# A DLRM tower on one core: in the first block all 26 tables are gathered, and lookups begin with the second block

## The chip, the cores and the metric

One core of one Trainium2 chip. The metric is the device time of one execution in microseconds, the median over timed runs. The core's engines are TensorE (PE in the profile), VectorE (DVE), ScalarE (ACT), GpSimd (POOL) and SyncE (SP), which run their own instruction streams and meet at semaphores.

## The reference, cut to what matters

```python
# ids: [2048, 26]; tables f: [V_f, 128], V_f = 1000 (seven of them), 1250, 12500 or 125000
e = stack([tbl_f[ids[:, f]] for f in range(26)], axis=1)          # [2048, 26, 128]
combined = concatenate((dense[:, None, :], e), axis=1)            # [2048, 27, 128]
inter = einsum('bfd,bgd->bfg', combined, combined)
pairs = inter[:, iu, ju]                                          # 351 pairs f < g
h = concatenate([dense, pairs, dense], axis=1)                    # [2048, 607]
h = maximum(h @ W_top1 + b_top1, 0.0)                             # 512
h = maximum(h @ W_top2 + b_top2, 0.0)                             # 256
y = h @ W_top3                                                    # [2048, 1]
```

Everything is float32.

## The kernel before, in words

The batch of 2048 is cut into 16 tiles of 128 samples; two tiles are a block (JT = 2, eight blocks). For each tile the kernel needs 27 slots in the tile `feats`: column 0 is the dense features, then seven small tables (1000 rows each), then nineteen large ones. Each slot holds, transposed, 128 dimensions by 128 samples.

The two kinds of table reach `feats` on different ways.

- Small tables, by lookup. The whole table is loaded once to SBUF (`load_table`, L181) in 125 partitions of eight rows, and split by ScalarE (`round_table`, L254) and VectorE (L391) into a rounded part `table_hi` and a remainder `table_lo`. For each block and small table, VectorE makes a one-hot tile of 1000 rows by 256 samples (`one_hot`, L338 to L345) from ids that SP has broadcast to all partitions (`load_wanted`, L174). TensorE multiplies the table with it in 16 matmuls (`look_up`, L419 to L432: eight chunks, two parts), and ScalarE copies the result from the PSUM bank `look` to `feats` (`empty_lookup`, L258). That makes 56 lookups (8 blocks x 7). There is one `look` bank, so lookup v waits until lookup v - 1 has been read; there are two one-hot tiles.
- Large tables, by gather. POOL issues one indirect DMA per tile and table (L248), 304 in all. It lands 128 rows, one per sample, in a slot of `rows`. Four gathers (at the end of a tile three) make a chunk, five chunks a tile, and chunk q = 5t + k uses slot q % 12. From the twelfth chunk on POOL waits until the chunk that held the slot has been turned (L246). TensorE turns a chunk with one transpose per table into a `turn` bank (`turn_rows`, L434 to L442; two banks), and ScalarE copies the bank to `feats` (`empty_turn`, L265).

The order of the work is written out by hand on each engine; there is no planner. Ahead of the tiles stands a start (PE at L497 to L502, ScalarE at L302 to L309, VectorE at L388 to L395, SP at L199 to L217): for k = 0 to 6 a table is rounded and looked up for block 0, and from k = 1 to 5 chunk k - 1 of tile 0 is turned between two lookups. So the start holds seven lookups and five chunks. SP issues the loads of the first four tables with their wanted ids, then the dense features of tile 0, part of W_top1, the other three tables, more wanted ids, and last the remaining weights. A load of wanted ids from the fifth on waits until an earlier one-hot has been made (L176), and everything behind it in SP's queue waits too. The raw tables land in the space of feature tiles 2 and 3.

Then follow 16 tiles of four segments each. In segment s of tile t TensorE does `products` (L444; 16 matmuls of 128 by 108, eight groups per bank), then one chunk of tile t + 1 (in the fourth segment two, L50), then in seven of the eight segments of a pair of tiles one lookup for the next block (`lookup_at`, L66), and one part of the MLP of tile t - 1: in segment 1 the pairs are turned (L461), in segment 2 and 3 the first and second layer (L469, L481), in segment 0 of the tile after that the third (L490). ScalarE reads products, chunks and lookups in the same order (`read_products`, L278). Products of a tile wait in segment 0 for all chunks and lookups of the tile and its dense column (L446 to L449). In the last two tiles there are no lookups; the last gather is issued during tile 12.

Of the kernel before, what the change touches and what calls it, by code (L numbers as in the profile page):

```python
# [7 lines left out]
I32 = mybir.dt.int32  # L8
# [19 lines left out]
ORDER = (0,) + tuple(1 + f for f in SMALL) + tuple(1 + f for f in LARGE)  # L28
LOOKUPS = BLOCKS * NS

# [35 lines left out]
def lookup_at(t, s):  # L66

    u = SEGS * (t % 2) + s
    return (t // 2 + 1) * NS + u if u < NS and t // 2 + 1 < BLOCKS else None


def arrivals(q):

    return sum(16 * CHUNK[i % NC][1] for i in range(q % SLOTS_OF_ROWS, q + 1, SLOTS_OF_ROWS))


def tower_program(nc, gather_ids, small_ids, dense_cols, dense_rows, small_tables, large_tables,
                  w_pairs, w_dense, w_dense2, w2, w3, b1, b2, y):
    ctx = ExitStack()
    with ctx:  # L80
# [3 lines left out]
        def sem(name):  # L84
            return ctx.enter_context(nc.semaphore(name))
# [9 lines left out]
        one = sb("one", [CP, 1])  # L95
        ids = sb("ids", [P, TILES, NG], I32)
        ident = sb("ident", [P, P])
        diag = [sb(f"diag{i}", [P, GROUPS * SLOTS]) for i in range(2)]
# [19 lines left out]
        ids_first_in = sem("ids_first_in")  # L118
        ids_rest_in = sem("ids_rest_in")
        gathered = [sem(f"gathered{i}") for i in range(SLOTS_OF_ROWS)]  # L120
        wanted_in = [sem(f"wanted_in{i}") for i in range(WANTED)]
# [41 lines left out]
        def raw_table(k):  # L163
            at = (2 + k % RAW // 2) * FT + k % 2 * CH * D
            return feats[0:CP, at:at + CH * D]

        def tail_bank(n):
            return prod[n // SEG_BANKS][:, (n % SEG_BANKS) * BANK:(n % SEG_BANKS) * BANK + P]
# [4 lines left out]
        def _(sp):  # L173
            def load_wanted(v):  # L174
                if v >= WANTED:
                    sp.wait_ge(onehot_ready, v - WANTED + 1)  # L176
                sp.dma_start(wanted[v % WANTED][:, :],
                             small_ids[v // NS:v // NS + 1, v % NS, :].broadcast_to([P, BS]))\
                    .then_inc(wanted_in[v % WANTED], 16)
# [53 lines left out]
        def _(gp):  # L233
# [5 lines left out]
            gp.wait_ge(ids_first_in, 16)  # L239
            for t in range(TILES):  # L240
                if t == 1:
                    gp.wait_ge(ids_rest_in, 16)
                for k, (g, m) in enumerate(CHUNK):
                    q = NC * t + k
                    if q >= SLOTS_OF_ROWS:
                        gp.wait_ge(turn_full, q - SLOTS_OF_ROWS + 1)  # L246
                    for f in range(m):
                        gp.indirect_dma_start(rows[:, q % SLOTS_OF_ROWS, f * D:(f + 1) * D], None, large_tables[g + f],  # L248
                                              bass.IndirectOffsetOnAxis(ap=ids[:, t, g + f:g + f + 1], axis=0))\
                            .then_inc(gathered[q % SLOTS_OF_ROWS], 16)  # L250

        @block.scalar
        def _(act):
# [4 lines left out]
            def empty_lookup(v):  # L258
                act.wait_ge(look_full, v + 1)
                at = v // NS % 2 * JT * FT  # L260
# [4 lines left out]
            def empty_turn(t, k):  # L265
                q, (g, m) = NC * t + k, CHUNK[k]
                act.wait_ge(turn_full, q + 1)
                nc.scalar.activation(slots_of(t)[:, 1 + NS + g:1 + NS + g + m, :],  # L268
                                     turn[q % 2][:, 0:m * P].rearrange("d (f b) -> d f b", f=m), ACT.Copy)\
                    .then_inc(turn_read, 1)  # L270
# [39 lines left out]

            for t in range(TILES):
                for s in range(SEGS):
# [3 lines left out]
                    if t + 1 < TILES:  # L316
                        for k in TURNS_AT[s]:
                            empty_turn(t + 1, k)
                        if s == 1:
                            place_dense(t + 1)  # L320
# [16 lines left out]
        def _(dve):  # L337
# [80 lines left out]
        def _(pe):  # L418
# [14 lines left out]

            def turn_rows(t, k):  # L434
                q, (g, m) = NC * t + k, CHUNK[k]
                pe.wait_ge(gathered[q % SLOTS_OF_ROWS], arrivals(q))
                if q >= 2:
                    pe.wait_ge(turn_read, q - 1)
                for f in range(m):
                    last = nc.tensor.transpose(turn[q % 2][:, f * P:(f + 1) * P],  # L440
                                               rows[:, q % SLOTS_OF_ROWS, f * D:(f + 1) * D], ident[:, :])
                last.then_inc(turn_full, 1)  # L442

            def products(t, s):  # L444
                m = SEGS * t + s
                if s == 0:  # L446
                    pe.wait_ge(turn_read, NC * (t + 1))
                    pe.wait_ge(look_read, NS * (t // 2 + 1))
                    pe.wait_ge(dense_placed, t + 1)  # L449
# [48 lines left out]
            pe.wait_ge(pads_ready, FEAT_TILES)  # L498
            for k in range(NS):
                look_up(k)  # L500
                if 1 <= k <= NC:
                    turn_rows(0, k - 1)  # L502

            for t in range(TILES):
                for s in range(SEGS):
# [3 lines left out]
                    if t + 1 < TILES:  # L509
                        for k in TURNS_AT[s]:  # L510
                            turn_rows(t + 1, k)
                    if (v := lookup_at(t, s)) is not None:
# [89 lines left out]
```

## Time and profile before

| | |
|---|---|
| median of three timed runs | 576.89 us (573.42 to 577.21) |
| profiled execution, its own time | 581.66 us |
| its span | 579.8 us |
| mean granted TensorE clock | 0.85 of full |
| busy PE, PEld, DVE, ACT, POOL | 407.9, 390.1, 212.6, 218.8, 297.6 us |
| matmuls | 3104 |
| DMA | 34.36 MB, mean 59 GB/s |

The profile shows one execution. PE is TensorE's matmul row, PEld its weight loads. A row of the timeline reads: start in us, duration in us, engine, line of the kernel, instruction, output<-input, count, and in brackets the idle time ahead of it and who ended it. Ends of matmuls are modelled. "remote" and "another core or an unknown queue" stand for a releaser that the profile could not name. A window over several instructions merges neighbours of one kind. Idle time of an engine off the critical path costs nothing.

### The profile page before, as it was taken

What the parts mean: (1) busy time and instruction counts of PE and PEld (TensorE: products, weight loads), DVE (VectorE), ACT (ScalarE), POOL (GpSimd) and SP (SyncE); (2) the same over time, 40 slices, a digit from 0 to 9 for tenths busy, and PEclk for the clock granted to TensorE, in tenths of its full rate; (3) what the DMA queues carried; (4) which work ended last, traced back from release to release, by engine and by line L of the source; (5) the groups of instructions that cost most, each with busy time, mean ns of one, the idle gap of its engine ahead of it and who ended that gap; (6) DMA issues with size and microseconds to landing.
All of it is one profiled execution on the core that took longest, in us unless ns stands there. A gap on an engine that the chain in (4) does not pass through costs nothing.

```text
span 579.8 us, 8030 instructions
## 1 busy us (share of the span) xinstructions
PE 407.9 (70%) x3104; PEld 390.1 (67%) x3104; DVE 212.6 (37%) x603; ACT 218.8 (38%) x452; POOL 297.6 (51%) x311
## 2 busy tenths in 40 slices
PE   1503027667859495987969595986949595899997
PEld 1502027667859495976859494976849494899995
DVE  5502027233434324453434323443433423371122
ACT  1201024444334342444335341444334352455641
POOL 5777746575555646474555636475554646400000
PEclk9766559897969788896979799896969898799998
DMA  8922215222112222222122212221121222100000
GB/s 190 245 63 59 54 35 167 64 68 55 53 48 55 52 53 56 55 69 52 45 63 54 57 49 59 51 69 51 46 60 50 50 57 63 41 6 1 2 1 1
DMA packets 24935, 34.36 MB, mean 59 GB/s; under 512 B 8808, under 2 KB 18552, under 8 KB 24898
## 3 DMA queue, kind: packets, MB, share of 16 engines
q0 software_dynamic: 9728, 19.94, 14.0%
q1 hardware_dynamic: 13090, 13.76, 9.1%
q8 instruction: 25, 0.41, 0.3%
q10 hardware_dynamic: 2080, 0.16, 0.3%
q14 instruction: 12, 0.10, 0.1%
HBM read 33.82 MB, written 0.01 MB: 58 GB/s over the span
## 4 chain that ended last, share of the span: by engine, by line
PE 58%; another core or an unknown queue 22%; ACT 9%; issue 8%; DMA 2%; DVE 1%; SPq 0%
PE prod L456 19%; PE look L429 19%; PE mlp L474 7%; PE mlp L485 4%; PE turn L440 4%; ACT feats L268 3%; ACT diag L283 3%; PE mlp L476 2%; DMA dense<-in_dense_rows 2%; ACT feats L261 1%; PE mlp L466 1%; PE prod L535 1%; ACT table_hi L256 1%; ACT y_sb L296 0%
## 5 line engine op out<-in xcount | busy, mean ns | idle before, releaser
L248 POOL DMA_INDIRECT rows<-in_tbl,ids x304 | 296.8, 976 | 206.9 <-PE turn L440 78.6
L429 PE MATMUL look<-onehot,table_hi 125*128 125x256 f32 x448 | 137.9, 334 | 138.6 <-ACT feats L261 105.6
L343 DVE TENSOR_SCALAR onehot<-wanted,row_no 125x256 fp32r<-125x256 int32 x448 | 132.9, 368 | 186.4 <-remote 150.4
L429 PEld LDWEIGHTS look<-onehot,table_hi 125*128 125x128 f32 x448 | 103.5, 231 | 144.0 <-issue 144.0
L456 PE MATMUL prod<-feats 128*128 128x108 f32 x1024 | 133.6, 283 | 16.5 <-issue 11.2
L283 ACT ACTIVATE diag<-prod 32x216 f32<-32x216 f32 x256 | 87.7, 343 | 148.4 <-PE prod L456 137.6
L456 PEld LDWEIGHTS prod<-feats 128*128 128x128 f32 x1024 | 127.2, 200 | 19.4 <-issue 11.7
L429 PE MATMUL look<-onehot,table_lo 125*128 125x256 f32 x448 | 131.9, 321 | 0.0
L429 PEld LDWEIGHTS look<-onehot,table_lo 125*128 125x128 f32 x448 | 104.1, 232 | 0.0
L268 ACT ACTIVATE feats<-turn 128x512 f32<-128x512 f32 (+1 forms) x80 | 79.5, 1032 | 41.7 <-remote 25.4
L261 ACT ACTIVATE feats<-look 128x256 f32<-128x256 f32 x56 | 34.9, 624 | 139.5 <-remote 116.1
L366 DVE TENSOR_SCALAR h<-mlp,b_sb 128x128 f32<-128x128 f32 x90 | 26.0, 345 | 147.9 <-PE mlp L476 101.8
L440 PE MATMUL turn<-ident,rows 128*128 128x128 f32 x304 | 48.7, 282 | 12.3 <-issue 12.3
L474 PE MATMUL mlp<-pairs_t,w_sb 117*128 117x128 f32 x360 | 50.2, 275 | 0.2 <-ACT pairs_t L290 0.2
L440 PEld LDWEIGHTS turn<-ident,rows 128*128 128x128 f32 x304 | 36.4, 147 | 17.8 <-issue 17.7
L474 PEld LDWEIGHTS mlp<-pairs_t,w_sb 117*128 117x128 f32 x360 | 45.0, 191 | 0.5 <-ACT pairs_t L290 0.4
L352 DVE STREAM_TRANSPOSE table<-diag 128x864 f32<-128x864 f32 x16 | 31.5, 1969 | 0.0
L485 PE MATMUL mlp<-h,w_sb 128*128 128x128 f32 x240 | 29.3, 275 | 0.0
L485 PEld LDWEIGHTS mlp<-h,w_sb 128*128 128x128 f32 x240 | 28.0, 192 | 0.0
L476 PE MATMUL mlp<-dense,w_sb 128*128 128x128 f32 x120 | 23.2, 274 | 0.0
L476 PEld LDWEIGHTS mlp<-dense,w_sb 128*128 128x128 f32 x120 | 18.2, 191 | 0.0
L391 DVE TENSOR_TENSOR table_lo<-feats,table_hi 125x1024 fp32r<-125x1024 f32 x7 | 8.6, 1227 | 19.7 <-issue 11.3
(39 smaller groups left out, 96.9 us busy)
## 6 DMA issues: line engine op xcount, KB each, us to landing
wanted<-in_small_ids SPq DMA_DIRECT2D x56, 128.0 KB
rows<-in_tbl,ids POOLq DMA_INDIRECT x304
feats<-in_tbl SPq DMA_DIRECT2D x7, 448.0 KB
dense<-in_dense_rows SPq DMA_DIRECT2D x16, 64.0 KB
w_sb<-in_w_pairs SPq DMA_DIRECT2D x1, 702.0 KB
w_sb<-in_w SPq DMA_DIRECT2D x1, 512.0 KB
feats<-in_tbl SPq DMA_DIRECT2D x7, 52.0 KB
w_sb<-in_w_dense SPq DMA_DIRECT2D x1, 256.0 KB
```

The costliest lines, as they stand in the source:

```text
L248: gp.indirect_dma_start(rows[:, q % SLOTS_OF_ROWS, f * D:(f + 1) * D], None, large_tables[g + f], bass.IndirectOffsetOnAxis(ap=ids[:, t, g ...
L261: nc.scalar.activation(feats[:, at:at + JT * FT].rearrange("d (b w) -> d w b", w=W)[:, 1 + v % NS, :], look[:, 0:BS], ACT.Copy)\
L268: nc.scalar.activation(slots_of(t)[:, 1 + NS + g:1 + NS + g + m, :], turn[q % 2][:, 0:m * P].rearrange("d (f b) -> d f b", f=m), ACT.Copy)\
L283: last = nc.scalar.activation(diag[t % 2][W * i:W * (i + 1), s * SEG_GROUPS * SLOTS:(s + 1) * SEG_GROUPS * SLOTS], prod_part(prod[s % 2], ...
L343: made = nc.vector.tensor_scalar(onehot[v % 2][:, c, :], wanted[v % WANTED][0:CP, :], row_no[:, c:c + 1], None, ALU.is_equal)
L352: nc.vector.transpose(by_row[:, :, 0:SLOTS].rearrange("p i j -> p j i"), diag[t % 2][:, :].rearrange("p (n j) -> p j n", j=SLOTS)).then_in ...
L429: last = nc.tensor.matmul(look[:, 0:BS], part[:, k, c * D:(c + 1) * D], onehot[v % 2][:, c, :], start=(c == 0 and part is table_hi), stop= ...
L440: last = nc.tensor.transpose(turn[q % 2][:, f * P:(f + 1) * P], rows[:, q % SLOTS_OF_ROWS, f * D:(f + 1) * D], ident[:, :])
L456: last = nc.tensor.matmul(prod[s % 2][:, to:to + GS * SLOTS], own, own.rearrange("d (s w) -> d s w", w=W)[:, :, 0:SLOTS], start=True, stop ...
L474: nc.tensor.matmul(mlp[:, n * P:(n + 1) * P], w1_sb[0:PR, c * H1 + n * P:c * H1 + (n + 1) * P], pairs_t[:, c * P:(c + 1) * P], start=(c == ...
L476: last = nc.tensor.matmul(mlp[:, n * P:(n + 1) * P], w1_sb[:, PC * H1 + n * P:PC * H1 + (n + 1) * P], dense[t % DENSE][:, :], start=False, ...
L485: last = nc.tensor.matmul(mlp[:, n * P:(n + 1) * P], w2_sb[:, c * H2 + n * P:c * H2 + (n + 1) * P], h1[:, c * P:(c + 1) * P], start=(c == ...
```

## The change

Lookups for block 0 are gone (`LOOKUPS` = 49, `lookup_at` numbers them from block 1). For tiles 0 and 1 POOL gathers the seven small tables as well, after the nineteen large ones: seven chunks a tile (4, 4, 4, 4, 3, 4, 3) in place of five. The list `CHUNKS` numbers all chunks in order; tiles 2 to 15 keep five. Two new loads on ScalarE's queue bring the ids of the small tables for tiles 0 and 1, one sample per partition. TensorE's start is seven chunks, each into a bank of its own: the two `turn` banks, the four halves of the `prod` banks, and `look`. ScalarE's start rounds all seven tables, places the dense column and empties the seven chunks. In tile 0 the chunks of tile 1 are spread over the segments as 1, 2, 2, 2; later tiles keep 1, 1, 1, 2. The loads of wanted ids in the start are three in place of ten. ScalarE waits before it empties the first lookup until all tables have been split, since the raw tables lie in the same space.

```diff
-LOOKUPS = BLOCKS * NS
+LOOKUPS = (BLOCKS - 1) * NS
...
-CHUNK = tuple((g, min(TB, NG - g)) for g in range(0, NG, TB))
-NC = len(CHUNK)
+FIRST_OF_LARGE = tuple((1 + NS + g, min(TB, NG - g)) for g in range(0, NG, TB))
+FIRST_OF_SMALL = tuple((1 + k, min(TB, NS - k)) for k in range(0, NS, TB))
+def chunks_of(t):
+    return FIRST_OF_LARGE + FIRST_OF_SMALL if t < JT else FIRST_OF_LARGE
+CHUNKS = tuple((t, *chunk) for t in range(TILES) for chunk in chunks_of(t))
...
-TURNS_AT = ((0,), (1,), (2,), tuple(range(3, NC)))
+def turns_at(t, s):
+    first, n = chunks_before(t), len(chunks_of(t))
+    ends = [n * (i + 1) // SEGS for i in range(SEGS)]
+    return range(first + (ends[s - 1] if s else 0), first + ends[s])
...
+        START_BANKS = [turn[0][:, :], turn[1][:, :], prod[0][:, 0:BANK], prod[0][:, BANK:], prod[1][:, 0:BANK],
+                       prod[1][:, BANK:], look[:, :]]
...
             for k in range(RAW):
-                load_wanted(k)
                 load_table(k)
+                if k < WANTED - 1:
+                    load_wanted(k)
...
             for k in range(RAW, NS):
-                load_wanted(k)
                 load_table(k)
-            for v in range(NS, NS + WANTED - 1):
-                load_wanted(v)
...
+            for q, (t, first, m) in enumerate(CHUNKS):
+                if q == chunks_before(1):
                     gp.wait_ge(ids_rest_in, 16)
+                if first < 1 + NS:
+                    gp.wait_ge(first_small_ids_in, 16 * JT)
+                if q >= SLOTS_OF_ROWS:
+                    gp.wait_ge(turn_full, q - SLOTS_OF_ROWS + 1)
+                for f in range(m):
+                    k = first - 1 + f
+                    rows_wanted = first_small_ids[:, t, k:k + 1] if k < NS else ids[:, t, k - NS:k - NS + 1]
+                    gp.indirect_dma_start(rows[:, q % SLOTS_OF_ROWS, f * D:(f + 1) * D], None,
+                                          (small_tables + large_tables)[k],
+                                          bass.IndirectOffsetOnAxis(ap=rows_wanted, axis=0))\
+                        .then_inc(gathered[q % SLOTS_OF_ROWS], 16)
...
+                if v == 0:
+                    act.wait_ge(lo_ready, NS)
...
+            for t in range(JT):
+                act.dma_start(first_small_ids[:, t, :], small_ids[0, :, t * P:(t + 1) * P].rearrange("k p -> p k"),
+                              allow_slow_non_contiguous=True).then_inc(first_small_ids_in, 16)
...
-            round_table(0)
+            for k in range(NS):
+                round_table(k)
             place_dense(0)
-            for k in range(NS):
-                if k + 1 < NS:
-                    round_table(k + 1)
-                empty_lookup(k)
-                if 1 <= k <= NC:
-                    empty_turn(0, k - 1)
+            for q in range(chunks_before(1)):
+                empty_turn(q)
...
             for k in range(NS):
-                one_hot(k)
+                if k == 1:
+                    one_hot(0)
                 dve.wait_ge(hi_ready, k + 1)
...
-            one_hot(NS)
...
                 pe.wait_ge(gathered[q % SLOTS_OF_ROWS], arrivals(q))
-                if q >= 2:
+                if q >= len(START_BANKS):
                     pe.wait_ge(turn_read, q - 1)
...
-            for k in range(NS):
-                look_up(k)
-                if 1 <= k <= NC:
-                    turn_rows(0, k - 1)
+            for q in range(chunks_before(1)):
+                turn_rows(q)
```

## Rows read from the trace of the kernel before

**Rows 1.** The page's slices: busy tenths in 40 slices of 14.5 us
```profile
PE   1503027667859495987969595986949595899997
...
POOL 5777746575555646474555636475554646400000
```

**Rows 2.** The costliest group of the page: busy, mean ns | idle before, releaser
```profile
L248 POOL DMA_INDIRECT rows<-in_tbl,ids x304 | 296.8, 976 | 206.9 <-PE turn L440 78.6
```

**Rows 3.** Stretches: length, busy (instructions) of PE, PEld, DVE, ACT, POOL, clock, DMA share, GB/s
```profile
5.30:30.00 24.70, 10.61 (x56) 10.02 (x56) 13.53 (x35) 5.92 (x8) 19.22 (x19) 0.86 0.99 242
30.00:75.30 45.30, 4.59 (x20) 4.24 (x20) 4.89 (x10) 2.84 (x4) 34.59 (x36) 0.56 0.22 57
...
185.40:218.00 32.60, 24.75 (x188) 23.79 (x187) 12.04 (x36) 12.84 (x27) 17.76 (x19) 0.84 0.21 54
...
513.20:535.30 22.10, 21.43 (x189) 20.86 (x187) 9.33 (x28) 12.75 (x27) 0.00 (x0) 1.00 0.00 1
```

**Rows 4.** Timeline of PE, 24 to 94 us
```profile
26.33 0.36 PE L429 MATMUL look<-onehot,table_hi 125*128 125x256 f32 x1 [0.71 <-issue]
...
28.32 0.60 PE L440 MATMUL turn<-ident,rows 128*128 128x128 f32 x4
44.78 0.55 PE L429 MATMUL look<-onehot,table_hi 125*128 125x256 f32 x1 [15.85 <-ACT feats L261]
...
82.65 0.55 PE L429 MATMUL look<-onehot,table_hi 125*128 125x256 f32 x1 [33.28 <-ACT feats L261]
...
93.36 2.01 PE L456 MATMUL prod<-feats 128*128 128x108 f32 x16 [0.75 <-issue]
```

**Rows 5.** Timeline of ACT, 29 to 82 us
```profile
29.30 1.05 ACT L256 ACTIVATE table_hi<-feats 125x1024 fp32r<-125x1024 f32 x1
44.02 0.61 ACT L261 ACTIVATE feats<-look 128x256 f32<-128x256 f32 x1 [13.67 <-remote]
53.84 1.02 ACT L268 ACTIVATE feats<-turn 128x512 f32<-128x512 f32 x1 [9.21 <-issue]
...
81.89 0.62 ACT L261 ACTIVATE feats<-look 128x256 f32<-128x256 f32 x1 [26.17 <-remote]
```

**Rows 6.** Timeline of POOL: gathers 1, 20, 26, 52 and 55
```profile
5.30 1.10 POOL L248 DMA_INDIRECT rows<-in_tbl,ids  x1 [3.72 <-DMA ids<-in_gather_ids]
...
30.94 1.49 POOL L248 DMA_INDIRECT rows<-in_tbl,ids  x1 [0.30 <-issue]
...
38.98 0.94 POOL L248 DMA_INDIRECT rows<-in_tbl,ids  x1 [0.30 <-issue]
...
71.82 0.94 POOL L248 DMA_INDIRECT rows<-in_tbl,ids  x1 [0.30 <-issue]
...
82.18 0.95 POOL L248 DMA_INDIRECT rows<-in_tbl,ids  x1 [6.92 <-remote]
```

**Rows 7.** Timeline of PE, ACT and POOL in tile 3, 181 to 200 us
```profile
181.84 1.60 POOL L248 DMA_INDIRECT rows<-in_tbl,ids  x1 [4.25 <-PE turn L440]
...
187.82 0.66 PE L440 MATMUL turn<-ident,rows 128*128 128x128 f32 x4
...
188.23 0.37 PE L429 MATMUL look<-onehot,table_hi 125*128 125x256 f32 x1
...
192.31 1.03 ACT L268 ACTIVATE feats<-turn 128x512 f32<-128x512 f32 x1 [2.57 <-remote]
...
199.43 0.61 ACT L261 ACTIVATE feats<-look 128x256 f32<-128x256 f32 x1 [6.09 <-remote]
...
199.89 1.05 POOL L248 DMA_INDIRECT rows<-in_tbl,ids  x1 [2.59 <-remote]
```

**Rows 8.** The chain that ended last: first and last of nine pieces alike
```profile
159.92 6.07 another core or an unknown queue
...
487.73 6.07 another core or an unknown queue
```

**Rows 9.** Gathers issued up to the first product of tile 2 (POOL alone)
```profile
0.00:151.30 151.30, 95.81 (x97) 0.77 0.39 97
```

**Rows 10.** DMA issues: queue, count, KB, median us to landing
```profile
ids<-in_gather_ids ACTq DMA_DIRECT2D x1, 142.5 KB, 6.0
```

More of the change, by code:

```diff
@@ L46, with chunks_before @@
 TB = 4
-CHUNK = tuple((g, min(TB, NG - g)) for g in range(0, NG, TB))
-NC = len(CHUNK)
-SLOTS_OF_ROWS = 12
-TURNS_AT = ((0,), (1,), (2,), tuple(range(3, NC)))
+FIRST_OF_LARGE = tuple((1 + NS + g, min(TB, NG - g)) for g in range(0, NG, TB))
[3 more added lines that the diff above has]
+CHUNKS = tuple((t, *chunk) for t in range(TILES) for chunk in chunks_of(t))
+SLOTS_OF_ROWS = 12
+def chunks_before(t):
+    return sum(len(chunks_of(i)) for i in range(t))
+def turns_at(t, s):
+    first, n = chunks_before(t), len(chunks_of(t))
+    ends = [n * (i + 1) // SEGS for i in range(SEGS)]
+    return range(first + (ends[s - 1] if s else 0), first + ends[s])
 PAIRS = SLOTS * (SLOTS - 1) // 2
@@ L68, in lookup_at @@
     u = SEGS * (t % 2) + s
-    return (t // 2 + 1) * NS + u if u < NS and t // 2 + 1 < BLOCKS else None
+    return t // 2 * NS + u if u < NS and t // 2 + 1 < BLOCKS else None
 def arrivals(q):
-    return sum(16 * CHUNK[i % NC][1] for i in range(q % SLOTS_OF_ROWS, q + 1, SLOTS_OF_ROWS))
+    return sum(16 * CHUNKS[i][2] for i in range(q % SLOTS_OF_ROWS, q + 1, SLOTS_OF_ROWS))
 def tower_program(nc, gather_ids, small_ids, dense_cols, dense_rows, small_tables, large_tables,
@@ L96, in tower_program @@
         ids = sb("ids", [P, TILES, NG], I32)
+        first_small_ids = sb("first_small_ids", [P, JT, NS], I32)
         ident = sb("ident", [P, P])
@@ L119, in tower_program @@
         ids_rest_in = sem("ids_rest_in")
+        first_small_ids_in = sem("first_small_ids_in")
         gathered = [sem(f"gathered{i}") for i in range(SLOTS_OF_ROWS)]
@@ L165, in raw_table, with turn_bank @@
             return feats[0:CP, at:at + CH * D]
+        START_BANKS = [turn[0][:, :], turn[1][:, :], prod[0][:, 0:BANK], prod[0][:, BANK:], prod[1][:, 0:BANK],
+                       prod[1][:, BANK:], look[:, :]]
+        def turn_bank(q):
+            return START_BANKS[q] if q < len(START_BANKS) else turn[q % 2]
         def tail_bank(n):
@@ L239, in _ @@
             gp.wait_ge(ids_first_in, 16)
-            for t in range(TILES):
-                if t == 1:
+            for q, (t, first, m) in enumerate(CHUNKS):
+                if q == chunks_before(1):
                     gp.wait_ge(ids_rest_in, 16)
[L243 to L250, printed above, removed]
+                if first < 1 + NS:
[9 more added lines that the diff above has]
+                        .then_inc(gathered[q % SLOTS_OF_ROWS], 16)
         @block.scalar
@@ L263, in empty_lookup, with empty_turn @@
                     .then_inc(look_read, 1)
-            def empty_turn(t, k):
-                q, (g, m) = NC * t + k, CHUNK[k]
+            def empty_turn(q):
+                t, first, m = CHUNKS[q]
                 act.wait_ge(turn_full, q + 1)
-                nc.scalar.activation(slots_of(t)[:, 1 + NS + g:1 + NS + g + m, :],
-                                     turn[q % 2][:, 0:m * P].rearrange("d (f b) -> d f b", f=m), ACT.Copy)\
+                nc.scalar.activation(slots_of(t)[:, first:first + m, :],
+                                     turn_bank(q)[:, 0:m * P].rearrange("d (f b) -> d f b", f=m), ACT.Copy)\
                     .then_inc(turn_read, 1)
@@ L316, in _ @@
                     if t + 1 < TILES:
-                        for k in TURNS_AT[s]:
-                            empty_turn(t + 1, k)
+                        for q in turns_at(t + 1, s):
+                            empty_turn(q)
                         if s == 1:
@@ L432, in look_up, with turn_rows @@
                 last.then_inc(look_full, 1)
-            def turn_rows(t, k):
-                q, (g, m) = NC * t + k, CHUNK[k]
+            def turn_rows(q):
+                t, first, m = CHUNKS[q]
                 pe.wait_ge(gathered[q % SLOTS_OF_ROWS], arrivals(q))
-                if q >= 2:
+                if q >= len(START_BANKS):
                     pe.wait_ge(turn_read, q - 1)
                 for f in range(m):
-                    last = nc.tensor.transpose(turn[q % 2][:, f * P:(f + 1) * P],
+                    last = nc.tensor.transpose(turn_bank(q)[:, f * P:(f + 1) * P],
                                                rows[:, q % SLOTS_OF_ROWS, f * D:(f + 1) * D], ident[:, :])
@@ L446, in products @@
                 if s == 0:
-                    pe.wait_ge(turn_read, NC * (t + 1))
-                    pe.wait_ge(look_read, NS * (t // 2 + 1))
+                    pe.wait_ge(turn_read, chunks_before(t + 1))
+                    if t >= JT:
+                        pe.wait_ge(look_read, NS * (t // JT))
                     pe.wait_ge(dense_placed, t + 1)
@@ L509, in _ @@
                     if t + 1 < TILES:
-                        for k in TURNS_AT[s]:
-                            turn_rows(t + 1, k)
+                        for q in turns_at(t + 1, s):
+                            turn_rows(q)
                     if (v := lookup_at(t, s)) is not None:
```

4 lines of the change are left out of this document (2 added, 2 removed).

## The prediction

> **What bounds the kernel now.** The profiled execution took 581.66 us around a span of 579.8; the median of the three timed runs is 576.89 (573.42 to 577.21), so the profile lies 0.8% above it. I sum against the profile and subtract 4.8 us at the end.
>
> I read the slices first [rows 1]: from the third slice to the fifth (29 to 72 us) POOL is at 5 to 7 tenths and more while PE reads 0, 3, 0. The costliest group [rows 2] is the gathers: 304 of 976 ns, the largest busy sum of any engine but PE. The stretches [rows 3] put this in order: up to 30 us DMA moves 242 GB/s; from 30.0 to 75.3 POOL issues 36 gathers and PE does 20 matmuls; then PE finishes the lookups; tile 0 starts at 93.4, tile 1 at 119.4, tile 2 at 151.3 (the starts of the first products of each, as at the end of [rows 4]).
>
> Why does PE do nothing for 45 us? The reader should follow PE's and ScalarE's rows side by side [rows 4, 5]. Lookup 2 starts on PE at 26.33 with matmuls some 0.12 us apart, and the four transposes that follow it start at 28.32. ScalarE, idle, reads that lookup at 44.02 and the transposes at 53.84. Lookup 3 starts at 44.78, right after that first reading, and is itself read at 81.89. Nothing is queued that explains it: data and buffers are there. The gathers [rows 6] go on every 1.25 us from 5.30 until 75.26 (82.18 less 6.92), 54 of them, and then wait for turned rows. 6.6 us after the last one the pending results are read, and lookups 4 to 6 take the 10.7 us from 82.65 to 93.36 [rows 4].
>
> The same pattern returns in every tile. Around 190 us [rows 7] 12 gathers run from 181.84 to 197.3 (199.89 less 2.59). The transposes that PE starts at 187.82 are read at 192.31, the lookup started at 188.23 is read at 199.43, 2.1 us after the run of gathers ended. Waits of that kind, 6.06 to 6.11 us each and put down to an unknown queue, stand nine times in the chain that ended last [rows 8]. And tile 13, in which there are no gathers left, takes 22.1 us for 189 matmuls; tile 3, with 188 matmuls and 19 gathers, takes 32.6 [rows 3]. So what PE has finished is seen late while gathers run without a pause: not in the first 6 or 7 us of a run, increasingly afterwards, until the run ends. This is my reading of what sets the time at the start and in each tile. The Trainium skill ("Perfetto Trace Analysis", Tensor Engine Instruction) adds that a matmul's reported end is an estimate, and that its semaphore follows only when PSUM has acknowledged the bytes; so PE's own row cannot show such a delay, as is the case here.
>
> **The change, part by part.**
>
> Lookups removed. Seven of the 56 go. Lookups 0 to 3 lie under the table loads or under the long run of gathers, so they give nothing back by themselves. Lookups 4 to 6 lie after the release: from 82.65 to the first product at 93.36 [rows 4] is the 10.7 us. Minus 10.7. The one-hots go with them (VectorE) and so do seven reads on ScalarE, both on no path of their own.
>
> Gathers added: seven tables for two tiles, 14 gathers, 318 in all. Their price has two ends. The low end is the steady one: (32.6 - 22.1) / 19 = 0.55 us each [rows 3], 7.7 in all. The high end is full serial time, 1.25 each [rows 6], 17.5 in all. I take the high end, because the added gathers lie in the start, where the run of gathers is long and PE's work is all but stopped: 20 matmuls in 45.3 us against 188 in 32.6 [rows 3]. By POOL's count, the kernel before has issued 97 gathers when tile 2 begins [rows 9]; the new one needs some 14 more for the same place. Plus 17.5.
>
> Chunks added. Tiles 0 and 1 have seven chunks each in place of five: four more batches on PE (0.60) and four more copies on ScalarE (1.03) [rows 4, 5]. Some overlap; I take 0.9 each. Plus 3.5 (0 to 6.5).
>
> Seven banks for tile 0. PE no longer waits for turn_read there. It hardly waited for it before, and what is late is the news of the transposes, not a bank. Nothing (0 to -2).
>
> Window of 12 chunk slots. This is what makes the start no shorter. POOL stops only when the twelfth chunk ahead is not yet turned. Before, two turned chunks were seen and it issued 54 gathers (10 chunks 38, two 8, two 8). Now the first 12 chunks hold 45 gathers. With four chunks seen it issues 60, with all seven of tile 0 it issues 71, and every one turned early prolongs the run. At (75.26 - 5.30)/54 = 1.30 each, that is an end at 83 or at 97 us, and PE is heard again some 7 us later: 90 or 104. In the first case tile 0's products start at about 93, as now; in the second they start early (about 50) but one segment of four is done by 104. The seven batches then turned in tile 0 release 27 gathers in place of 19, so that its stalls are longer too. Both roads give tile 1 some 8 to 15 us later than 119.4, which agrees with the sum.
>
> Tables. They are loaded and rounded on ScalarE before it empties the first chunk: seven times 1.05 [rows 5]. Table loads no longer stand behind one-hots, and the MLP weights no longer wait until 85 us, so tables (7 of 0.512 MB), weights (1.7), the wanted ids and dense features (0.6) and 26 gathers (0.066 each) come to 7.6 MB, 31 us at the measured 242 GB/s [rows 3]. All tables are rounded by about 35, before the 26th gather ends at 39.9 [rows 6]; free under it, 0 to 3 otherwise.
>
> The new loads of ids have 1792 single words on ScalarE's queue. The comparable load of ids, 15 words a run, lands in 6.0 us [rows 10]; the first small gather is the 20th, at 30.94 [rows 6]. They are hidden; even at 20 us they would be. SP's queue: three wanted loads in place of seven, none waits long.
>
> Waits added: POOL for first_small_ids (met), ScalarE for lo_ready at lookup 7 (met by 37). Lookups of blocks 1 to 7, chunk sizes against the 12 slots from tile 2 on, and the tail are as before: nothing.
>
> Sum: -10.7 + 17.5 + 3.5 = +10.3, so 592.0 in a profile and 587 as a median.
>
> **Rivals.**
>
> (a) Gathers and PE do not disturb each other in the start. Then the 26th gather ends at 39.9, its rows are there a microsecond or two later, turning and emptying take 1.6, and tile 0's products start at about 44 in place of 93.4. Tile 1 needs the 52nd gather, which ends at 72.8 [rows 6], so it starts at about 76 in place of 119.4: 43 to 49 us gained, about 531. For it: PE's rows show every matmul done on time, and lookup 1's result must have been read by 26.33, when lookup 2 was let go, with gathers running since 5.30 [rows 4, 6]. Against it: the nine waits of [rows 8], and the idle 45 us. By the Trainium skill ("SBUF — State Buffer", Who interferes with whom) DMA never contends with a compute engine, which would leave only this rival. The trace differs: 10.5 us more for the same matmuls [rows 3].
>
> (b) The delay weakens because the new start asks little of PE. In a 12-gather run one lookup of 16 matmuls takes the 7.1 us from 192.31 to 199.43 [rows 7], 2.25 a microsecond. Were that the pace from 47 us on, tile 0's 154 matmuls (64 products, 64 in lookups, 26 transposes) would end at 115, 4 us before now; with the start's slack some 572.
>
> (c) The added gathers cost only the steady 0.55: -10.7 + 7.7 + 3.5 = +0.5, so 577, no difference. This is the case in which the three lookups that go are paid back by the gathers.
>
> (d) The new ids come late or the change does not reorder the start as it says: POOL would pause at the 20th gather. A pause helps PE, so even that is within 3 us.
>
> **How the numbers follow.** Forecast 0.48, (a) 0.18, (b) 0.13, (c) with (d) 0.21. The forecast's own range is 580 to 603. From all: 545 to 603, which leaves out most of (a) below. A measurement here can tell 1% (5.8 us) from nothing. Faster by more: (a), most of (b), 0.29. Within: most of (c) and the low end of the forecast, 0.21. Slower: 0.50.
>
> **What would show it.** Right: a run of 60 to 71 gathers from 5 us without a pause; chunks of tile 0 turned on PE by about 42 but the last ones read by ScalarE many microseconds later; PE below one matmul a microsecond until the run ends at 83 to 97; tile 1's products at 127 to 135; from tile 2 on the same 32 to 33 us a tile. Wrong: ScalarE emptying seven chunks by 45 us and tile 0's four segments done by 80, with the run of gathers still going. Then the delay needs something that the old start had and this one has not, the lookups above all, and (a) holds.

## The result, and the profile after

The changed kernel took 591.29 us in the median (589.14 to 593.1, four runs) against 577.05 for the kernel before beside it: 1.0258 times, 95% interval 1.0202 to 1.0313. Repeated later it took 591.47 against 578.62, 1.0224 (1.0189 to 1.0258). Forecast were 587, slower. The profiled execution has a span of 591.3 us, 11.5 more than before. On three of five occasions, these two among them, the kernel before took 573 to 579 us (called A below), on the other two 419 to 420 (called B); a kernel can't choose between them, and each run is compared with the kernel before of its own occasion unless the text says otherwise.

The page's slices of the changed kernel, which answer to [rows 1]:

```profile
PE   0235110736976959495959869495959778699997
...
POOL 6877776467564555646464645556464745500000
```

POOL stayed at 7 to the end of the fifth slice before, now to the end of the sixth and at 6 in the seventh. PE, which peaks at 5 in slice four, goes back to 1, 1, 0 behind it. The costliest group answers to [rows 2]; behind it stand the 14 gathers that were added:

```profile
L277 POOL DMA_INDIRECT rows<-in_tbl,ids x304 | 297.8, 979 | 201.7 <-issue 80.5
...
L277 POOL DMA_INDIRECT rows<-in_tbl,first_small_ids x14 | 13.2, 944 | 4.3 <-issue 4.3
```

The stretches of the changed kernel, cut at its own tile starts, answer to [rows 3]:

```profile
0.00:43.20 43.20, 7.35 (x26) 4.58 (x26) 16.35 (x30) 15.59 (x17) 32.66 (x36) 1.00 0.83 193
43.20:101.00 57.80, 12.15 (x60) 10.16 (x60) 0.00 (x0) 2.39 (x5) 43.78 (x47) 0.60 0.20 53
101.00:135.10 34.10, 17.82 (x95) 16.23 (x95) 7.12 (x25) 11.71 (x23) 16.51 (x18) 0.60 0.17 44
...
199.30:231.10 31.80, 24.24 (x189) 22.92 (x188) 12.18 (x36) 12.88 (x27) 17.83 (x20) 0.89 0.22 56
526.40:548.50 22.10, 21.43 (x189) 20.86 (x187) 9.26 (x28) 12.75 (x27) 0.00 (x0) 1.00 0.01 2
```

The start is over at 43.2 us, 50 us earlier than before (93.4). Then come 57.8 us in which PE does 60 matmuls and POOL 47 gathers. Tile 0 ends at 135.1, where before it ended at 119.4. From there on both kernels go at nearly the same pace: tile 3 takes 31.8 us (32.6 before), tile 13 without gathers 22.1, exactly as before.

ScalarE's timeline in tile 0 answers to [rows 5]:

```profile
42.38 0.81 ACT L300 ACTIVATE feats<-look 128x384 f32<-128x384 f32 x1 [2.48 <-PE look L472]
51.23 1.40 ACT L315 ACTIVATE diag<-prod 32x216 f32<-32x216 f32 x4 [8.04 <-issue]
59.65 1.03 ACT L300 ACTIVATE feats<-turn 128x512 f32<-128x512 f32 x1 [7.01 <-remote]
104.44 0.62 ACT L293 ACTIVATE feats<-look 128x256 f32<-128x256 f32 x1 [43.76 <-remote]
```

All seven chunks are emptied by 43.2 and almost without delay: the last three transposes start at 41.44 and are read at 42.38. The first products are read at 51.23, the chunk behind them at 59.65, and the lookup behind that at 104.44. Its last matmul started at 49.41, and the trace records the semaphore that tells of it at 104.41, just before ScalarE starts: it is the news that is late, not ScalarE. PE's timeline tells the same from the other side (it answers to [rows 4]):

```profile
43.25 3.75 PE L489 MATMUL prod<-feats 128*128 128x108 f32 x16 [0.90 <-ACT feats L300]
46.79 0.98 PE L472 MATMUL turn<-ident,rows 128*128 128x128 f32 x4
...
49.53 1.37 PE L489 MATMUL prod<-feats 128*128 128x108 f32 x11
51.93 0.25 PE L489 MATMUL prod<-feats 128*128 128x108 f32 x1 [1.03 <-issue]
...
64.52 0.37 PE L472 MATMUL turn<-ident,rows 128*128 128x128 f32 x1 [3.16 <-issue]
66.62 0.37 PE L472 MATMUL turn<-ident,rows 128*128 128x128 f32 x1 [1.73 <-issue]
69.42 0.37 PE L472 MATMUL turn<-ident,rows 128*128 128x128 f32 x1 [2.43 <-issue]
```

After 49.53 even the starts are held back: single matmuls, 2.1 us apart at first, and between 66.62 and 83.42 six times 2.80 us apart, where otherwise 0.12 us lie between two. And POOL, the answer to [rows 6]:

```profile
100.05 0.94 POOL L277 DMA_INDIRECT rows<-in_tbl,ids  x1 [0.30 <-issue]
110.47 0.94 POOL L277 DMA_INDIRECT rows<-in_tbl,ids  x1 [9.48 <-remote]
```

The first run of gathers has 75 of them and ends at 101.0; the lookup is read 3.4 us later.

One thing more differs between A and B, and it is in the traces themselves. The first line is of the kernel before in A, the second of the same kernel with a shorter window in B (an experiment below); at the end stands the median time from issue to landing:

```profile
rows<-in_tbl,ids POOLq DMA_INDIRECT x304
rows<-in_tbl,ids POOLq DMA_INDIRECT x304, 2.5
```

In A the time is missing, because most of the recorded semaphore updates that it is read from are missing: from 43.2 to 101 us the changed kernel's trace has 100 of them, the same stretch of a variant in B (window of 7) 946. So in A the record of semaphores is thin while gathers run, and no landing of a gather can be read there. The DMA packets themselves are all there and no slower: the 9728 of the gathers take 14.0% of the 579.8 us before and 18.9% of 416.3 in B, 81 and 79 us.

### The profile page after: what moved, and what is told of

It is laid out like the page before. It is cut to its first block, busy times and chain, and to the rows that moved or that the text cites. A ratio compares the mean times of both kernels' runs of the same rounds, so it can differ in the third digit from the quotient of the medians.

```text
span 591.3 us, 7771 instructions
## 1 busy us (share of the span) xinstructions
PE 399.8 (68%) x3006; PEld 377.4 (64%) x3006; DVE 196.2 (33%) x547; ACT 218.7 (37%) x449; POOL 311.7 (53%) x325
## 4 chain that ended last, share of the span: by engine, by line
PE 50%; another core or an unknown queue 29%; ACT 9%; issue 6%; POOL 5%; DMA 1%; DVE 1%
PE prod L489 15%; PE look L461 15%; PE mlp L507 7%; POOL rows L277 5%; ACT feats L300 4%; PE mlp L518 4%; PE turn L472 3%; ACT diag L315 3%; PE mlp L509 2%; PE mlp L526 2%; ACT feats L293 1%; PE mlp L499 1%; ACT y_sb L328 1%; PE prod L566 0%
## 5 line engine op out<-in xcount | busy, mean ns | idle before, releaser
L375 DVE TENSOR_SCALAR onehot<-wanted,row_no 125x256 fp32r<-125x256 int32 x392 | 116.1, 368 | 222.7 <-remote 191.6
L461 PE MATMUL look<-onehot,table_hi 125*128 125x256 f32 x392 | 120.6, 334 | 97.3 <-ACT feats L293 82.2
L461 PEld LDWEIGHTS look<-onehot,table_hi 125*128 125x128 f32 x392 | 90.3, 230 | 104.9 <-issue 104.9
L489 PEld LDWEIGHTS prod<-feats 128*128 128x128 f32 x1024 | 128.6, 202 | 21.3 <-issue 13.5
L461 PE MATMUL look<-onehot,table_lo 125*128 125x256 f32 x392 | 115.6, 321 | 0.3 <-issue 0.3
L461 PEld LDWEIGHTS look<-onehot,table_lo 125*128 125x128 f32 x392 | 90.8, 232 | 1.1 <-issue 1.1
L300 ACT ACTIVATE feats<-turn 128x512 f32<-128x512 f32 (+1 forms) x79 | 78.1, 1034 | 32.2 <-remote 30.3
L472 PE MATMUL turn<-ident,rows 128*128 128x128 f32 x300 | 51.1, 287 | 54.2 <-issue 34.9
L293 ACT ACTIVATE feats<-look 128x256 f32<-128x256 f32 x49 | 30.6, 625 | 146.9 <-remote 132.6
L277 POOL DMA_INDIRECT rows<-in_tbl,first_small_ids x14 | 13.2, 944 | 4.3 <-issue 4.3
```

Source lines behind the costliest of these rows:

```text
L300: nc.scalar.activation(slots_of(t)[:, first:first + m, :], turn_bank(q)[:, 0:m * P].rearrange("d (f b) -> d f b", f=m), ACT.Copy)\
L375: made = nc.vector.tensor_scalar(onehot[v % 2][:, c, :], wanted[v % WANTED][0:CP, :], row_no[:, c:c + 1], None, ALU.is_equal)
L461: last = nc.tensor.matmul(look[:, 0:BS], part[:, k, c * D:(c + 1) * D], onehot[v % 2][:, c, :], start=(c == 0 and part is table_hi), stop= ...
L472: last = nc.tensor.transpose(turn_bank(q)[:, f * P:(f + 1) * P], rows[:, q % SLOTS_OF_ROWS, f * D:(f + 1) * D], ident[:, :])
L489: last = nc.tensor.matmul(prod[s % 2][:, to:to + GS * SLOTS], own, own.rearrange("d (s w) -> d s w", w=W)[:, :, 0:SLOTS], start=True, stop ...
```

## The experiments

**No gathers from chunk 12 on** (twice), and **clearings in their place** (twice). The output then rests on stale rows, and TensorE no longer waits for rows from chunk 12 on; the first 45 gathers stay. POOL clears the fourth column block of `rows` once at the start, some 2 us (in the kernels with clearings and with quarter rows too).

```diff
                 for f in range(m):
                     k = first - 1 + f
+                    if q >= 12:
+                        continue
...
-                pe.wait_ge(gathered[q % SLOTS_OF_ROWS], arrivals(q))
+                if q < SLOTS_OF_ROWS:
+                    pe.wait_ge(gathered[q % SLOTS_OF_ROWS], arrivals(q))
```

> Changed kernel; the gathers from chunk 12 on are left out (the rows turned from there on are stale ones), all else stays, and POOL clears one column block of rows first (about 2 us). 273 of 318 gathers go. Theory G (gathers running without a pause hold back what PE has finished): tile 0 starts by about 45 us, POOL's run ends near 60, every tile takes the 22 us that tile 13 took, total 400 to 430 us. Rival L (PE's own program, the lookups above all, sets the stalls): the tiles keep 30 us or more and the total stays above 540.

> Changed kernel without the gathers from chunk 12 on, for a chip on which the kernel before takes 577 us (414 where it took 419). Theories G and H: 410 to 420 us here too, since what disturbs is gone. Rival C (such a chip is slow in PE or its semaphores by itself): above 500.

Measured: 413.73 in B (kernel before 419.37) and 422.58 in A (kernel before 573.43). Without most gathers A and B differ by 2%; the kernel before, with all of its own, differs by 37%. The stretches of tiles 1 to 3 of the run in A:

```profile
82.40:103.90 21.50, 20.83 (x183) 20.64 (x183) 10.49 (x33) 12.81 (x27) 0.00 (x0) 1.00 0.08 23
103.90:127.20 23.30, 23.30 (x203) 22.92 (x204) 12.33 (x39) 13.30 (x28) 0.00 (x0) 1.00 0.11 26
127.20:149.30 22.10, 21.43 (x188) 20.86 (x186) 11.46 (x36) 12.78 (x27) 0.00 (x0) 1.00 0.08 22
```

These tiles take 21.5 to 23.3 us, like tile 13 with its 22.1, PE is busy for nearly all of it at the full clock, and lookups and one-hots are all there. So in A the stalls come with the gathers, and the rivals that put them on PE's own program (L) or on the setting by itself (C) fall. The 9 us that are left between A and B lie in tile 0, beside the end of the 45 gathers that stayed. It takes 41.2 us in A (first line) and 31.9 in B (second), and in A ScalarE reads the first products only at 66.96, 5.4 us after the last gather has ended (61.5):

```profile
41.20:82.40 41.20, 24.88 (x155) 23.92 (x155) 7.08 (x26) 13.59 (x28) 15.45 (x17) 0.75 0.14 39
41.70:73.60 31.90, 24.30 (x155) 23.62 (x155) 7.54 (x26) 14.42 (x28) 15.57 (x17) 0.89 0.19 52
66.96 1.40 ACT L319 ACTIVATE diag<-prod 32x216 f32<-32x216 f32 x4 [25.85 <-remote]
```

The trace in A has 62 recorded semaphore updates from 30 to 61.5 us, that in B 620; from 70 us on, without gathers, both are alike (1547 and 1507).

```diff
+                    if q >= 12:
+                        if made:
+                            gp.wait_ge(scratched, made)
+                        made += 1
+                        gp.memset(scratch[:, :], 0.0).then_inc(scratched, 1)
+                        continue
```

> As the kernel without gathers from chunk 12 on, but POOL clears a scratch tile of 128x620 in the place of each gather, about as long as one, under the same waits. If POOL's being busy is what disturbs (theory P: its instructions), the stalls come back: 540 to 600 us and long waits of ScalarE. If it is the DMA that POOL issues (theory D: descriptors or their traffic), the time is that of the kernel without the gathers, 400 to 430 us.

> Changed kernel with a clearing of 128x620 on POOL for each gather from chunk 12 on, for a chip on which the kernel before takes 577 us. Theory D (the DMA that POOL issues disturbs PE): 415 to 430 us. Theory P (POOL's being busy disturbs): 540 us or more.

Measured: 419.98 in B, 429.31 in A. In A the group, and tiles 1 and 2 (39 and 21 instructions on POOL):

```profile
L285 POOL MEMSET scratch<- 128x620 f32 x273 | 177.0, 648 | 113.5 <-PE turn L483 98.7
```

```profile
82.10:110.30 28.20, 22.96 (x182) 22.18 (x182) 23.14 (x37) 13.38 (x27) 24.03 (x39) 0.94 0.10 25
110.30:133.60 23.30, 23.28 (x202) 22.90 (x203) 19.15 (x39) 13.37 (x28) 13.28 (x21) 1.00 0.07 20
```

A clearing took 0.65 us, less than the 0.94 of a gather, but the clearings run in groups under the same waits (8 or 12, then 3 or 4, at a time), and tile 2 takes the same 23.3 us. Tile 1, in which POOL clears almost without a pause, takes 28.2 in place of 21.5; that is the whole difference to the kernel without gathers (429.31 to 422.58). At least half of it has another cause: PE waits 3.5 us for one-hots, which the clearings slow down. The longer of its two waits:

```profile
98.12 0.55 PE L471 MATMUL look<-onehot,table_hi 125*128 125x256 f32 x1 [2.53 <-DVE onehot L385]
```

So POOL's being busy (theory P) is not what costs 150 us and more; something that hangs on its gathers is (theory D). Whether that is their making on POOL, their traffic or their semaphore counts is not told apart. One rival stands that no run tests. Each execution here comes with the profiler's figures, so none shows the kernel without a profiler. A gather adds 16 semaphore updates to be recorded, and in A the record comes out thin exactly where PE's news is late. The taking of the record could be a part of the cause.

**A window of 7 chunks** (twice).

```diff
-                if q >= SLOTS_OF_ROWS:
-                    gp.wait_ge(turn_full, q - SLOTS_OF_ROWS + 1)
+                if q >= 7:
+                    gp.wait_ge(turn_full, q - 7 + 1)
```

> Changed kernel; POOL may be only 7 chunks ahead of the turned ones, not 12 (one number). The same 318 gathers. Theory G: the run in the start ends after 26 to 34 gathers (38 to 48 us), PE is heard in tile 0, tile 1 starts near 80 us in place of 135, and the later tiles change little: 530 to 560 us. Rival W (the window only matters as a store of rows, gathers are late when it is small): slower than 591, up to 620.

> Changed kernel with POOL at most 7 chunks ahead in place of 12, as before, for a chip on which the kernel before takes 577 us (there it took 434 where the kernel before took 419). Theory G (a run of gathers without a pause holds back PE's results, given such a chip): tile 1's products start near 80 us in place of 135, total 530 to 560 us. Rival W (small window makes gathers late): above 591. Rival H (on such a chip gathers and PE share one capacity whatever their order, so that only the sum counts): 580 to 600.

Measured: 434.35 in B (kernel before 419.37), 574.07 in A (573.43), one execution each. The 574 lie outside the range of G (530 to 560) and outside that of H (580 to 600). Tile 0 and tile 13 in A:

```profile
42.70:108.90 66.20, 28.59 (x155) 25.16 (x156) 7.12 (x24) 13.87 (x27) 43.22 (x47) 0.68 0.19 50
...
497.40:529.40 32.00, 24.22 (x188) 23.18 (x186) 9.91 (x28) 12.92 (x27) 15.76 (x17) 0.84 0.15 38
```

The first run is shorter (56 gathers, to 76.9 us) and tile 1 starts at 108.9 in place of 135.1, a gain of 26 us, though not at the 80 I had written. I had overlooked that the seven chunks of tile 0, all seen turned, let a window of 7 go on to 14 chunks, 52 gathers; one chunk of tile 1 seen turned added the other four. At the other end 10 us are given back, because gathers now reach into tile 13 (32.0 us in place of 22.1). What is left is 17 us below the 591 of the changed kernel, though measured on another occasion, and no difference to the kernel before. So with the same 318 gathers a shorter window takes the loss away in A.

In B the same kernel starts its first two tiles where rival (a) had put them:

```profile
40.50:74.90 34.40, 23.97 (x154) 22.94 (x155) 7.36 (x24) 14.57 (x27) 25.93 (x28) 0.86 0.25 66
...
217.70:240.90 23.20, 21.85 (x189) 21.00 (x187) 12.66 (x36) 13.11 (x27) 17.65 (x19) 1.00 0.27 75
```

Tile 0 starts at 40.5 and tile 1 at 74.9 (44 and 76 had been worked out), the products of 40.5 are read at 44.30, and still the kernel is 15 us slower than the one before. The page's chain says why:

```profile
POOL 70%; issue 22%; PE 5%; DMA 1%; DVE 1%; POOLq 0%; ACT 0%
```

Here POOL issues without a pause from 2.73 to 402.9 us, 318 gathers 1.25 to 1.26 us apart, and most of the chain is its issuing.

**Short lookups.** Each lookup keeps 2 of its 16 matmuls and each one-hot 1 of 8 parts.

```diff
-                for c in range(CH):
+                for c in range(1):
```

> Changed kernel; each lookup does 2 of its 16 matmuls and each one-hot 1 of its 8 parts (seven eighths of each small table are left out); waits and order stay. Theory G with a limited number of PE instructions let through during a run of gathers: the stalls shrink with the matmuls, a tile falls to 24 to 26 us, which is POOL's 19 x 1.25, total 470 to 500 us. If the stall hangs on the run of gathers alone and not on how much PE does, the tiles keep about 30 us, total 550 or more.

It ran in B: 432.75 against 419.37 for the kernel before and 434.35 for the window of 7 on the same occasion. With 686 matmuls fewer it gains 1.6 us on the window of 7, since POOL's 318 gathers last to 401 us there too. What it should have told of A stays open.

**Both kernels again.** No edit.

> The changed kernel as it is. In the first experiments the kernel before took 419 us in place of 577, and the kernel without gathers 414: on the chip of those runs PE is heard at once, gathers or not. If that holds on the chip of this run, rival (a) of the prediction applies to it: tile 0 starts at 43 in place of some 55 to 60 us, POOL's 52 gathers are done by 72, and the changed kernel is level with the kernel before or up to 10 us faster or slower (409 to 430). If this run falls where results are held back, it repeats 591 against 577.

> The kernel before as it is, for its profile. Where the kernel before takes 419 us: no wait of ScalarE for an unknown releaser above 3 us, tile 0's first products at 50 to 60 us, 22 to 25 us a tile, POOL's 19 gathers (24 us) the longest part of one. Where it takes 577: the profile already seen.

It fell on A and repeats the result: 591.47 against 578.62. The kernel before, one execution, took 573.04 with a first run of 50 gathers to 68.7 us and tile 1 at 118.8; the changed kernel again had a first run of 75, to 100.1 us, and tile 1 at 133.8. So the 15 to 16 us at the start of tile 1 are no accident of one execution. What comes behind it varies more: from tile 1's start to the end of the span the changed kernel won 4.2 us on the kernel before in the first pair of profiles and lost 4.9 in this one.

**The kernel before with a window of 6.**

```diff
-                    if q >= SLOTS_OF_ROWS:
-                        gp.wait_ge(turn_full, q - SLOTS_OF_ROWS + 1)
+                    if q >= 6:
+                        gp.wait_ge(turn_full, q - 6 + 1)
```

> Kernel before (lookups from block 0, 304 gathers) with POOL at most 6 chunks ahead of the turned ones in place of 12. Theory D (a long unbroken run of POOL's DMAs holds back PE) on a chip where the kernel before takes 577 us: the first run ends after 23 to 31 gathers (35 to 45 us) in place of 54 (75 us), tile 0 starts at 55 to 70 us in place of 93, tile 1 at 85 to 95 in place of 119; at the end about 10 us are lost, since gathers reach tile 13. Total 550 to 565 us. Rival W (late gathers): above 577. On a chip where the kernel before takes 419 us: 415 to 435.

It fell on B: 420.06 (418.2 to 421.27) against 419.79, ratio 1.0005 (0.9988 to 1.0023). There the window is of no account, because POOL never waits for it:

```profile
L248 POOL DMA_INDIRECT rows<-in_tbl,ids x304 | 288.6, 949 | 95.1 <-issue 92.1
```

```profile
4.25 1.10 POOL L248 DMA_INDIRECT rows<-in_tbl,ids  x1 [2.67 <-DMA ids<-in_gather_ids]
...
384.30 0.94 POOL L248 DMA_INDIRECT rows<-in_tbl,ids  x1 [0.30 <-issue]
```

304 gathers end at 385.2 us, 318 (window of 7, in B) at 402.9: 17.7 us for 14 gathers. In A this kernel was not tried, so whether the kernel before would gain there from a shorter window is open. This trace shows one thing more, the start of the kernel before in B:

```profile
42.70:60.40 17.70, 17.08 (x148) 16.88 (x148) 10.61 (x36) 12.27 (x26) 13.42 (x15) 1.00 0.42 107
```

Tile 0 starts at 42.7 and tile 1 at 60.4. The 50 us that the change wins at tile 0 are there only in A. In B the changed kernel (window of 7) starts tile 0 at 40.5, 2 us sooner, and tile 1 at 74.9, 14.5 us later, which is nearly all of its loss of 15.

**A quarter of each row**, and **plain loads in place of gathers**, both from chunk 12 on. (The first edit cuts the tables into rows of 32 and leaves the ids as they are, so it fetches the quarter row with that number, and not a quarter of the row that was wanted; bytes and counts are as said.)

```diff
-                    gp.indirect_dma_start(rows[:, q % SLOTS_OF_ROWS, f * D:(f + 1) * D], None,
-                                          (small_tables + large_tables)[k],
+                    gp.indirect_dma_start(rows[:, q % SLOTS_OF_ROWS, f * D:f * D + (D if q < 12 else D // 4)], None,
+                                          (small_tables + large_tables)[k] if q < 12 else
+                                          (small_tables + large_tables)[k].rearrange("v (a d) -> (v a) d", a=4),
```

```diff
+                    if q >= 12:
+                        gp.dma_start(rows[:, q % SLOTS_OF_ROWS, f * D:(f + 1) * D],
+                                     (small_tables + large_tables)[k][t * 32:t * 32 + P, :])\
+                            .then_inc(gathered[q % SLOTS_OF_ROWS], 16)
+                        continue
```

> Changed kernel; gathers from chunk 12 on fetch 32 of 128 columns (a quarter of the bytes, as many descriptors and semaphore counts; three quarters of each row are left stale). On a chip where the kernel before takes 577 us: if it is the bytes that disturb PE, stalls shrink and the total falls below 500; if it is descriptors, completions or POOL's way of issuing, it stays within 575 to 600.

> Changed kernel; from chunk 12 on POOL issues a plain load of 128 rows that lie together in place of each gather (same bytes, no list of ids). On a chip where the kernel before takes 577 us: if gathering by ids is what disturbs, the total falls to 420 to 480; if any DMA issued from POOL does it, the stalls stay and the total is 560 to 620 (a plain load may take POOL another time than 0.94 us).

Both fell on B too: 438.25 and 413.31 against 419.79. So which part of the gathers holds back PE in A (bytes, descriptors, counts on semaphores, the list of ids) is open. What they tell of B is the price of the gathers: a quarter of the bytes does not make one shorter, a plain load does.

```profile
L278 POOL DMA_INDIRECT rows<-in_tbl,ids x304 | 292.2, 961 | 92.9 <-issue 92.9
```

```profile
L278 POOL DMA_DIRECT2D rows<-in_tbl x273 | 147.3, 555 | 126.2 <-PE turn L477 122.7
```

The first group is of the quarter rows, the second of the plain loads. With 0.56 us a load POOL waits for PE again, and the total is that of the kernel without gathers (413.73).

## Why the prediction was right, point by point

- *PE's results are seen late while gathers run.* Held in A, and now shown there: 423 us without most of the gathers, 429 with clearings in their place, where the kernel before took 573 and the changed one, on other occasions, 591. In B it is not so, and the prediction, made from one trace in A, could not see that. "Not in the first 6 or 7 us of a run" did not hold as a rule: in the changed kernel the gathers had run for 40 us when the last chunk was read with no delay. The start asks PE for 26 transposes only, and it is with the first products that the delays begin. With it one of the signs that were to show the prediction right failed: the last chunks of tile 0 were to be read many microseconds late and were not. That was even the first half of the sign that was to show it wrong (seven chunks emptied by 45); its second half, tile 0's four segments done by 80, did not come. That a run of gathers lets only so many of PE's instructions through, and that a pause lets it catch up, would fit; it was not tested, since the short lookups ran in B.
- *The window of 12 makes the start no shorter.* This is what happened. Of the two roads the second was taken: all seven chunks are seen, tile 0 starts early (43.2, where 50 was given), and one segment of four is done when PE is heard again at 104.44 (104 was given). The first run has 75 gathers, four more than the 71 worked out, because a chunk of tile 1 was still seen turned at 59.65.
- *Tile 1 at 127 to 135.* It starts at 135.1, at the edge of what was given and 15.7 us late. In measured terms: the first run ends 25.7 us later (101.0 against 75.3), PE is heard 3.2 us sooner after it (3.4 against 6.6), and from there to tile 1 it takes 30.7 us (104.4 to 135.1) where it took 37.5 (81.9 to 119.4), so 6.8 are won. 25.7 - 3.2 - 6.8 = 15.7.
- *Lookups removed, -10.7.* The three lookups behind the first run did go, but no run takes out their share by itself. The 6.8 us hold both them and the 15 gathers (110.47 to 128.9) beside which tile 0 had to be finished (a lookup read at 130.31, after 10.5 us of waiting). In the second pair of profiles the same stretch won 14.0 us: the kernel before was released at 73.6 with more of its start still to do. So the term is neither confirmed nor corrected.
- *Gathers added, +17.5.* In B it is near: 17.7 us for the 14, and +13.4, +15.0 and +18.5 for the three variants with all 318. In A its size is luck. There the first run did not grow by 14 gathers but by 21 (54 to 75), 25.7 us, because the window reached further; and with a window of 7 the same 318 gathers cost nothing (574.07 against 573.43). What the term priced was the number of gathers, what A charged was how far POOL ran ahead. The prediction had that too, under the window of 12, but not in its sum.
- *Chunks added, +3.5.* Four times 0.9 are 3.6. All seven chunks of tile 0 are emptied by 43.2, under the run of gathers, so two of the four cost nothing that shows there; those of tile 1 were not measured by themselves.
- *The sum, +10.3.* The profiled pair differs by 11.5 us, the medians by 14.2 (577.05 to 591.29) and 12.9 (578.62 to 591.47). The 4.8 us that were taken off at the end hold for the profile before (581.66); the changed kernel's profiled execution (593.10) lies only 1.8 above its median. Direction and place (tile 1) come from the mechanism as forecast; that the total is so near is in part luck, since the terms of the sum are not what A added up.
- *Tables, ids, queues: nothing.* Held. The tables are rounded by 29.0, the 20th gather does not wait, all results of the start are read by 43.2. (The kernel before has ten loads of wanted ids in its start, not seven; priced at nothing, this changes no number.)
- *Rival (a)* gave the changed kernel's first two tiles in B to within 4 us (40.5 and 74.9 for 44 and 76), and still there is no gain. It compared them with the 93.4 and 119.4 of the kernel before in A; in B that kernel is at 42.7 and 60.4 (with a window of 6). Where PE is not held back, POOL's 1.25 us a gather sets the pace of the tiles, and the 14 more come before tile 1. The changed kernel itself was not run in B; its three variants with all 318 gathers took 434, 433 and 438 there against 419 to 420.
- *Rivals (b), (c), (d).* (b) had tile 0 end at 115 and 572 in all: it ended at 135.1. (c), 577 and no difference, is out for this kernel, though the window of 7 comes out like it. (d): POOL did not pause at the 20th gather.
- *The page's rule* that DMA never contends with a compute engine (the Trainium skill, "SBUF — State Buffer", Who interferes with whom) fits B, where the kernel with plain loads on POOL takes as long as the one without any (413.31 and 413.73). In A gathers do cost PE time, 423 us without most of them and 591 with all; but the rule speaks of ports, and no run here says by what road the gathers reach PE's results.

## What to carry to other kernels

Follow a gain at the start to the engine that paces the rest: 50 us sooner at tile 0 were worth less than nothing, as they were bought with work for the engine (POOL) that set the pace. Before a queue is let run ahead as far as its buffers reach, look at what the others do meanwhile; here a shorter window moved tile 1 by 26 us and took off 17 us in all. And check each term of a sum in the trace when the total fits: here the total was near and the largest term was not what had happened. Last, the kernel that one compares with may run in two ways; a gain that exists only beside one of them (here tile 0 at 93.4 or at 42.7) is no property of the change.

## What the runs showed of the hardware

- The same program took 420 us on some occasions and 577 on others, each within 1.5%, and the difference hangs on GpSimd's indirect DMAs: without most of them 414 and 423. What sets it is open; the number of the chip does not tell, since 3 stands beside one A and one B.
- In A the recorded semaphore updates are thin while gathers run (100 against 946 in B from 43.2 to 101 us), and as many as in B when none run. Whether this is a mark of the cause, or the recording a part of it, is open.
- In A TensorE can be cut down to one matmul in 2.80 us, with no wait that the profile shows, while GpSimd issues a gather every 1.25 us.
- A gather of 128 rows costs GpSimd 0.94 us and 0.30 to the next, with 512 or 128 bytes a row alike; a plain load of 128 rows 0.54 to 0.56.
- Clearings on GpSimd slow VectorE's one-hots beside them, from a mean of 349 ns in the kernel without gathers in A to 551. In the tile in which POOL cleared almost without a pause TensorE waited 3.5 us for them, and the tile took 28.2 us in place of 21.5.

```profile
L385 DVE TENSOR_SCALAR onehot<-wanted,row_no 125x256 fp32r<-125x256 int32 x392 | 187.6, 551 | 34.5 <-remote 34.2 <-PE look L471 0.3
```
